# Moving half of a weight conversion from the attention stage to GpSimd behind it, with smaller input transfers

## The reference

```python
x = x + tanh(g_xattn[0]) * xattn(layernorm(x), ctx, ctx)   # x 32x128x512, ctx 32x128x128
x = x + tanh(g_ffn[0])   * moe(layernorm(x), weights)
# xattn: 32 query heads over 8 key/value heads of width 16, softmax over 128 keys; no projections
# moe, for each of the 4096 tokens:
gate  = xt @ Wr + br                       # 7 routed experts; top 2 of gate + gate_bias
probs = softmax of the two chosen gates
u = xt @ Wup[e] + bup[e]                   # 512 x 512
g = silu(u @ Wgate[e] + bgate[e]) * u      # 512 x 512
y = g @ Wdown[e] + bdown[e]                # 512 x 512
out = sum over the two chosen e of probs * y, plus the same three layers of one shared expert for every token
```

## Time and profile before

| | us |
|---|---|
| median of 3 runs | 1272.61 (1270.43 to 1278.21) |
| span of the profiled execution | 1271.7 |
| attention (to the first `norm2`) | 0 to 352.5 |
| norm stage (to the first expert matmul) | 352.5 to 407.5 |
| expert tiles | 407.5 to the end |
| busy: PE 1197.0, DVE 852.9, ACT 585.5, POOL 382.3 | |

### The profile page before, as it was taken

How to read it: one execution, slowest core, us unless ns; L and a number is a source line. 1 busy time by engine, 2 the same in 40 slices (tenths; PEclk the granted TensorE clock), 3 DMA queues, 4 the chain that set the end, 5 groups by cost and what they waited for, 6 DMA issues and landing times.

```text
span 1271.7 us, 40424 instructions
## 1 busy us (share of the span) xinstructions
PE 1197.0 (94%) x15162; PEld 889.3 (70%) x15162; DVE 852.9 (67%) x1470; ACT 585.5 (46%) x1131; POOL 382.3 (30%) x454
## 2 busy tenths in 40 slices
PE   3878889999878999999999999999999999999998
PEld 2544444555467777778888888888888888877775
DVE  5889989999887789445554455444444444447899
ACT  2767779898797422233333333333333333322221
POOL 4466766676830000210111111111111111006752
PEclk9888999999989999999999999999999999999999
DMA  5675555656665132644322454215412233057875
GB/s 183 211 247 176 176 172 187 212 186 212 209 252 190 52 133 67 225 152 152 119 82 82 139 183 157 66 58 193 146 66 66 66 125 123 33 175 234 265 227 176
DMA packets 91043, 196.32 MB, mean 154 GB/s; under 512 B 12128, under 2 KB 12640, under 8 KB 90976
## 3 DMA queue, kind: packets, MB, share of 16 engines
q1 hardware_dynamic: 80256, 160.30, 36.8%
q0 software_dynamic: 10720, 35.14, 9.2%
HBM read 331.68 MB, written 64.49 MB: 312 GB/s over the span
## 4 chain that ended last, share of the span: by engine, by line
PE 73%; DVE 12%; issue 5%; POOL 3%; DMA 3%; ACT 2%; SPq 1%; DVEq 1%; ACTq 0%; POOLq 0%
PE PS L1671 40%; PE PS L1709 20%; DVE negm L1011 5%; PE PS L1632 3%; PE PS L1484 3%; DMA qB<-negT 2%; PE PS L1518 2%; PE PS L1504 1%; ACT x2n L881 1%; POOL whl L696 1%; PE PS L1532 1%; DMA wr<-in_wr 1%; PE PS L1526 1%; DVE X L1314 1%; DVE rec L1024 1%
## 5 line engine op out<-in xcount | busy, mean ns | idle before, releaser
L1671 PE MATMUL PS<-xT,wb 128*128 128x128 f16 (+1 forms) x4128 | 279.8, 229 | 2.3 <-DVE gate L1152 1.6
L1671 PE MATMUL PS<-uhl,wb 128*128 128x128 f16 (+1 forms) x4128 | 279.8, 229 | 1.2 <-DVE uhl L1265 1.2
L1671 PEld LDWEIGHTS PS<-xT,wb 128*128 128x128 f16 x4128 | 264.1, 98 | 11.2 <-DVE gate L1152 1.7
L1671 PEld LDWEIGHTS PS<-uhl,wb 128*128 128x128 f16 x4128 | 263.5, 98 | 10.1 <-DVE uhl L1265 1.4
L1709 PE MATMUL PS<-wb,ghl 128*128 128x512 f16 x1200 | 267.2, 379 | 0.0
L1709 PEld LDWEIGHTS PS<-wb,ghl 128*128 128x128 f16 x1200 | 115.9, 98 | 130.2
L926 ACT ACTIVATE sl<-PS,bb 128x128 f32<-128x128 f32 (+1 forms) x344 | 106.7, 387 | 187.5 <-PE PS L1671 187.5
L747 POOL COPY ixr<-idx 128x2 int32 (+1 forms) x35 | 6.4, 183 | 593.3 <-PE PS L1632 593.3
L916 ACT ACTIVATE u<-PS,bb 128x128 f32<-128x128 f32 (+1 forms) x344 | 106.6, 387 | 169.5 <-PE PS L1671 164.1
L1272 DVE TENSOR_TENSOR g<-sl,u 128x512 f32<-128x512 f32 x102 | 70.5, 691 | 150.2 <-ACT sl L926 150.1
L1011 DVE TENSOR_REDUCE negm<-PS 128x8 f16<-128x1024 f32 x128 | 155.2, 1213 | 23.8 <-PE PS L1484 23.0
(11 more groups left out here) (161 smaller groups left out, 1375.9 us busy)
## 6 DMA issues: line engine op xcount, KB each, us to landing
wb<-wsc SPq DMA_DIRECT2D x219, 1024.0 KB
wst<-in_wall SPq DMA_DIRECT2D x32, 768.0 KB, 6.0
wsc<-whl SPq DMA_DIRECT2D x32, 768.0 KB, 4.3
ysl<-yb SPq DMA_DIRECT2D x43, 512.0 KB
bd<-in_bdown SPq DMA_DIRECT2D x74, 256.0 KB
X<-in_x SPq DMA_DIRECT2D x8, 1024.0 KB, 6.7
qB<-qT SPq DMA_DIRECT2D x32, 256.0 KB, 2.7
xnd<-xhl SPq DMA_DIRECT2D x32, 256.0 KB, 2.0
```

Source lines behind the costliest of these rows:

```text
L1671: ins = pe.matmul(bank_of(bank, t, m, kind), wb[:, j, l, k, w, m * P:(m + 1) * P], rhs(x, k)[:, ts], start=(n == 0), stop=(n == len(TERMS) ...
```

## The change

- Only 15 blocks (`DURING`) are converted in attention, one in every second body. Times 64 goes from DVE to POOL there (`weights64` in odd bodies), the high piece stays on ACT (odd bodies), the low piece on POOL (even bodies).
- The other 17 blocks are converted after attention by POOL alone (`late_block`: times 64, cast, subtract), through new tiles `wst2` and `whl2` that lie where `wb` buffer 1 will be. SP loads two of them ahead, and stores and loads between the `store_x2` of groups 2 to 7 (one block each) and between the tiles 0 to 4 (2, 2, 2, 2, 3 blocks).
- Buffer 1 of `wb` is therefore needed later: tiles 0 to 6 use buffer 0 and tile 7 buffer 1; the shared expert's second load and the first routed expert's loads move back by a tile or more.
- X arrives in 16 transfers of 2 batches (512 KB) where there were 8 of 4; the pairs from the sixth on are issued one in each body. ctx arrives in three transfers where there were two.

```diff
+XP = NB // 2
+DURING = NB // 2 - 1
+KEPT_C = (0, 4, 14, NB)
...
+        with ExitStack() as spare:
+            sb("first_half", [P, 3 * KT * 2 * HID], F16, spare)
+            wst2 = sb("wst2", [P, 2, 3, HID], F32, spare)
+            whl2 = sb("whl2", [P, 2, 3, 2, HID], F16, spare)
...
             if kind == "early":
-                return 1 if isinstance(half, int) and half == SH_A // 2 - 1 else 0
+                return 1 if isinstance(i, int) and i == SH_A - 1 else 0
...
+                    sp.dma_start(X[:, 2 * c:2 * c + 2, :], xv[:, 2 * c:2 * c + 2, :]).then_inc(x_in[c], 16)
...
-                if isinstance(half, int) and number(half, par) + 3 < XC:
-                    load_rows([number(half, par) + 3])
-                if not start:
-                    pv = (half - 1, 1) if par == 0 else (half, 0)
-                    store_w(*pv, nx is None)
+                if isinstance(half, int) and number(half, par) + 5 < XP:
+                    load_rows([number(half, par) + 5])
+                if isinstance(half, int) and number(half, par) == 5:
+                    load_ctx(2)
+                if par == 1 and not (isinstance(half, int) and half == 0):
+                    store_w(half, quad)
...
+            sp.wait_ge(S["t_done"], UNITS * NB)
+            for n in range(DURING, DURING + 2):
+                load_late(n)
+            late = iter(range(DURING, NB))
+            for i in range(NB // 4):
                 store_x2(i)
+                if i > 1:
+                    store_late(next(late))
...
+                for n in range(0, 0 if i == 5 else 3 if i == 4 else 2):
+                    store_late(next(late))
+                if i == 5:
+                    for j in range(2):
+                        sp.wait_ge(w_out[j], 16 * (NB // 2))
+                    for l in range(3):
+                        first_layer(l, 1)
                 store_y(i, i % 2)
...
+            def late_block(n):
+
+                j = n % 2
+                g.wait_ge(w_in[j], 16 * (n // 2 + 1))
+                g.tensor_scalar(wst2[:, j, :, :], wst2[:, j, :, :], WS, None, ALU.mult).then_inc(S["w64_ready"], 1)
+                g.wait_ge(S["w64_ready"], n + 1)
+                g.wait_ge(w_out[j], 16 * (n // 2))
+                g.tensor_copy(whl2[:, j, :, 0, :], wst2[:, j, :, :]).then_inc(S["whi_ready"], 1)
+                g.wait_ge(S["whi_ready"], n + 1)
+                g.tensor_tensor(whl2[:, j, :, 1, :], wst2[:, j, :, :], whl2[:, j, :, 0, :], ALU.subtract).then_inc(S["wlo_ready"], 1)
...
-                if not start:
-                    weights_lo(*pv)
+                if par == 0 and not start:
+                    weights_lo(half - 1, 1 - weight_block(half, quad)[0])
+                if par == 1 and not (isinstance(half, int) and half >= DURING):
+                    weights64(half, quad)
...
             residual(NB // 2 - 1, 1)
-            weights_lo(NB // 2 - 1, 1)
+            g.wait_ge(S["pv_done"], 2 * NB)
+            late_block(DURING)
             rstd2(3)
+            for n in range(DURING + 1, NB):
+                late_block(n)
...
-                weights64(half, par)
```

More of the change, by code:

```diff
@@ L201, in program @@
         qB_in = [sem(f"qB_in{j}") for j in range(2)]
-        x_in = [sem(f"x_in{c}") for c in range(XC)]
-        c_in = [sem(f"c_in{c}") for c in range(2)]
+        x_in = [sem(f"x_in{c}") for c in range(XP)]
+        c_in = [sem(f"c_in{c}") for c in range(3)]
         w_in = [sem(f"w_in{j}") for j in range(2)]
@@ L369, in neg_rows, with stored_block, store_w, load_late @@
                 sp.dma_start(qB[D::STRIP, par, pair, :, :], negT[:, pair, :]).then_inc(neg_in[pair], 16)
[L371 to L378, removed]
+            def stored_block(n, pieces, j):
+                sp.wait_ge(S["wlo_ready"], n + 1)
+                sp.dma_start(wsc[bass.ds(block_of(n), 1)].rearrange("o l p r -> (o p) l r"),
+                             pieces[:, j, :, :, :].rearrange("p l h c -> p l (h c)")).then_inc(w_out[j], 16)
+            def store_w(half, quad):
+                j = 1 - weight_block(half, quad)[0]
+                stored_block(half - 1, whl, j)
+                if not (isinstance(half, int) and half + 1 >= DURING):
+                    load_w(half + 1, j)
+            def load_late(n):
+                sp.dma_start(wst2[:, n % 2, :, :], a["wall"][block_of(n)]).then_inc(w_in[n % 2], 16)
+            def store_late(n):
+                stored_block(n, whl2, n % 2)
+                if n + 2 < NB:
+                    load_late(n + 2)
             queries_again(0, 0, 0)
@@ L821, in evac_o, with weights_hi @@
                 act.activation(oT[:, hf, :], AT, ACT.Copy).then_inc(S["oT_ready"], 1)
[L823 to L829, removed]
+            def weights_hi(half, quad):
+                j, count = weight_block(half, quad)
+                act.wait_ge(S["w64_ready"], half + 1)
+                need(act, w_out[j], count)
+                act.activation(whl[:, j, :, 0, :], wst[:, j, :, :], ACT.Copy).then_inc(S["whi_ready"], 1)
             act.wait_ge(S["vone"], 7)
@@ L851, in body @@
                 exps(half, par, 0)
-                if isinstance(half, int) and number(half, par) == 1:
-                    act.wait_ge(c_in[1], 16)
+                for c in (1, 2):
+                    if isinstance(half, int) and number(half, par) == KEPT_C[c] - 3:
+                        act.wait_ge(c_in[c], 16)
                 if later is not None:
@@ L865, in body @@
                 exps(half, par, 3)
-                if not (isinstance(half, int) and number(half, par) == NB - 1):
-                    weights_hi(half, par)
+                if par == 1 and not (isinstance(half, int) and half >= DURING):
+                    weights_hi(half, quad)
             over_batches(act, body)
@@ L960, in stats1 @@
             def stats1(c):
-                v.wait_ge(x_in[c], 16)
+                for pair in range(2 * c, 2 * c + 2):
+                    v.wait_ge(x_in[pair], 16)
                 for b in range(c * n, (c + 1) * n):
@@ L969, in late_stats1 @@
             def late_stats1(c, pair, one):
-                if pair == 0 and one == 0:
-                    v.wait_ge(x_in[c], 16)
+                if one == 0:
+                    v.wait_ge(x_in[2 * c + pair], 16)
                 b = c * n + 2 * pair + one
```

72 lines of the change are left out of this document (33 added, 39 removed).

## The result

| | before | after |
|---|---|---|
| median, us | 1271.52 (4 runs, 1270.21 to 1278.21) | 1364.62 (4 runs, 1363.22 to 1368.31) |
| ratio | | 1.0713, 95% interval 1.0677 to 1.0748 |
| attention | 352.5 | 338.6 (-13.9) |
| norm stage | 55.0 | 93.8 (+38.8) |
| tiles 0 to 5, up to the gate of tile 6 | 110.2 | 175.5 (+65.3) |

The change makes the kernel 7.1% slower. The direction, and where the time goes, are as forecast (-18, +19, +28), but the amount is 90 us of span (93 between the medians) and not 29. The boundaries are read from the timeline: the first `norm2` on ACT, the first expert matmul on PE, and PE's gate products of tile 6. The profiled stretches are one run each. In the ratios of this document executions far above the rest are left out (one of small_rows_lo_thirds, 2299.6 us, and one of the kernel before beside it, 2908.2).

What follows compares the result with a forecast made beforehand. Early attention was taken as bound by waits, its loop by nearly full PE, DVE and ACT, the norm stage by ACT, expert tiles by PE. Forecast: 1271.7 - 18 + 19 + 28 = 1300.7, stated as 1300 us; range 1256 to 1330.

Steps and rivals of the forecast that it cites:

- Small transfers, -4: Attention, early bodies: smaller X and ctx transfers shorten waits for negT, body 5 gets a new pile; -4 us (-10 to +1).
- Early pairs, -10: Attention, six pairs of bodies up to the twelfth: key split and DVE's chain shorten without DVE's times 64; 6 x 1.7 = -10.
- the loop, -4: Attention, other 16 bodies: DVE relieved, but PE nearly full, so 0.25 us gained a body; -4 (0 to -11).
- What one late block costs, 1.5 + 1.5 + 3.1: POOL behind attention: times 64, cast and subtraction of one block take 6.1 us, 17 blocks 104 us.
- Rival (c): POOL's one-operand instructions cost 3.1 like the subtraction, a block 9.3, DVE loses half as much again; 1329 us, chance 0.15.
- What it costs DVE: Behind attention: DVE's two-SBUF-operand instructions stop until POOL's instruction ends, extrapolated from 0.5 us waits to whole 3.1 us instructions.
- Norm stage, +19: Norm stage: a group with a block becomes 3.4 us longer by blocking, about 5.5 blocks; +19 (+9 to +28).
- Tiles, +28: Tiles 0 to 4: a block costs DVE about 4.5 us, less DVE's idle time, all passed to PE; +28 (+12 to +45).
- Routed tiles and the later reloads, 0: After the late blocks: tile 7's weights and the routed loads have a tile of cover each; +0, at most +3.
- POOL would keep ahead of SP: SP's queue: with 6.1 us a block, POOL finishes late blocks before SP's queued stores need to wait for them.
- (a): Behind attention: blocking is no loss, POOL falls into DVE's idle and PSUM time, only transfers count; 1263 us, chance 0.16.
- (b): No blocking loss, attention at its better bound (-28) as the clock rises, transfers hidden (+3); 1247 us, chance 0.12.

Runs made afterwards that it cites:

- small_rows_lo_thirds: Kernel before with small X and ctx transfers, all times 64 on POOL in two-operation form, low-piece subtraction cut in thirds: 1277.0 us, ratio 1.0018.
- fast64: The change with POOL's times 64, in attention and behind it, in the two-operation form (times 64, plus 0.0) on one row of 1536: 1329.2 us.
- late_empty: The change with each late block's three POOL instructions shrunk to two columns, all transfers kept, last 17 blocks stored as zeros: 1273.6 us.

## Why the prediction was wrong in its amount

Each step against what it measured:

- **Small transfers, -4.** By themselves 0.6 in the profile; the runs leave -4.1 to +1.5, so that -4 is at the edge of what they allow. The pile that I had put on body 5 came: the chain of the changed kernel has one transfer of `negT` left in the early bodies, of 7.31 us, in that body.
- **Early pairs, -10, and the loop, -4.** Attention gained 13.9 for a forecast of 18. The loop alone gave more than its term: 8.84 us a body (252.10 - 216.73 over 4), where I had 9.0, so 16 x 0.4 = 6.4. The other 7.5 lie in the early bodies (by POOL's thirteenth addition to X, at 181.33 and before at 188.61, the change is 7.3 ahead), and not 14. Both shares are of one run and known to a few us. The key split fell to 0.40 as I had said.
- **What one late block costs, 1.5 + 1.5 + 3.1.** This is the step that failed first: times 64 took 4.2, outside the bounds of 1.4 to 3.1. I had priced it by the memset, because "both read one operand" (a memset reads none), and took the subtraction as an upper bound, because it reads two. Neither bounds it. fast64 puts its weight at 34 us. Rival (c) had half of the mechanism: it made both one-operand instructions cost 3.1, where times 64 cost 4.2 and the cast 1.5. That its block of 9.3 us is near the measured 9.1 is luck, and its 1329 was still too low for a measured 1364.6. The Trainium skill's rule for one input (GPSIMD Engine Reference, "4.1 Engine selection"), by which a block was to stay near 6.1, holds for the cast and the two-operation form and not for this one.
- **What it costs DVE: it stops until POOL's instruction is over.** Right, and so was the extrapolation to a whole long instruction: 3.47 for 0.69 beside a POOL subtraction of 3.15. It is not exact for the slow times 64, beside which DVE was done 0.33 us before the end, twice.
- **Norm stage, +19.** Measured +38.8, made of 14.8 for the transfers, 11.0 for blocking with a block of 6.6 us, and 13.0 more with the slow times 64. I had worked out both blocking (19) and transfers (9) and took the larger, as if one hid the other. It does not: fast64 grew by 25.8, which is more than the 14.8 of the transfers and more than the 17.1 us that DVE stood (64.1 - 47.0). They do not add up in full either, as far as DVE's 17.1 is the measure of blocking; a run with blocking and no transfers is missing. The transfers alone were under-sized, 9 for 14.8. DVE's loss was over-sized, 17.1 / 7 = 2.4 us a block in fast64 for my 4.0, and the blocks were seven and not 5.5. The 13.0 are the size of times 64 again.
- **Tiles, +28.** Measured +65.3, of which 43.9 (154.7 - 110.9, from late_empty) remain in fast64. The share that I gave to DVE was nearly right: 4.5 of each 6.1 us, 45 for ten blocks; measured 137.8 - 88.5 = 49.3. What failed is the way from DVE's loss to the stretch. I took nine blocks, subtracted DVE's idle time (12.6 us over tiles 0 to 4), and had no term for PE's clock. By the table above PE's waits in fast64 grew by 30.7, which is near my 28 (32.4 with the tenth block), and 13.9 more are PE's own products, which take longer behind each wait. So one account is that the idle time did cover what I said and the missing term is the clock. Seen from DVE it is another: in all five kernels the stretch grew by about what DVE stood, and its idle time in the stretch hardly fell (21.6 before, 16.9 in fast64), as if it bought little, since a stop in front of `uhl` shifts PE, PE shifts ACT, and DVE waits again. Slower products also leave DVE more idle time, and no run holds the clock up, so which of the two it is stays open. What is shown is the sum, DVE's added time almost one to one, and the clock's 13.9 in it, which the prediction put at nothing.
- **Routed tiles and the later reloads, 0.** Right: 753.7 against 754.0.

That transfers for tile 7 were covered and that blocking is what decides the sign held. That POOL would keep ahead of SP held but for two blocks in the tiles, for which SP waited 7.6 and 15.1 us (5.1 and 12.6 in fast64); no wait of PE is put down to it. Of the signs, `low2` above 2 us came, the groups of the norm stage took about 11 us and not 9 (POOL's times 64 at 401.70, 412.49 and 423.59), and tile 2, from gate to gate, 32.6 and not 24. Rivals (a) and (b) are out by late_empty against the change: 91 us apart with the same transfers. Still open is why the one-operation form is slow, and how the 7.5 us of the early bodies divide between keys and DVE.

## What to carry to other kernels

- Spare time on GpSimd is not spare if VectorE works from SBUF at the same time. Price a moved instruction by what VectorE loses while it runs. In a stage that is a loop of PE, ACT and DVE waiting for each other, count that loss almost in full: here the stage grew by about what VectorE stood, and a part of that was TensorE's slower clock behind each wait (13.9 of 44.6 us in fast64). A block brought about 0.8 us where it was taken out (13.9 / 17, small transfers included), and cost 3.7 (norm stage, 25.8 / 7, its transfers included) to 4.4 (tiles, 43.9 / 10) where it was put, even in its fast form.
- An instruction that the trace does not show need not be bounded by a neighbour that does more work. Measure it first; one run with four forms would have shown the factor of 2.6.
- Where such work must lie beside VectorE, cut it in short pieces on the engine that has time (16 us here), and do not take the larger of transfers and blocking for the whole: 25.8 us here, with 14.8 for the transfers alone and 17.1 that VectorE stood.

## What the runs showed of the hardware

- GpSimd's tensor_scalar with one operation on 1536 float32 columns takes 4.1 to 4.4 us whatever its shape, type of output (4.24 into float16) or source of the factor. With a second operation it takes 1.48 to 1.54 in attention and 1.62 to 1.70 behind it, as fast as the cast (1.53 to 1.66), and faster than the product with a broadcast tile (2.90).
- VectorE's two-input subtraction ended 0.54 to 0.55 us after a GpSimd addition or subtraction that it had to wait for (0.69 grew to 3.47), but 0.33 us before the end of the one-operation `tensor_scalar`, twice.
- A GpSimd instruction that only writes leaves VectorE's two-input instructions alone (694 and 703 ns beside it) and holds up its casts (526 ns for 426).
- VectorE gets in between GpSimd instructions that stand back to back, and then GpSimd waits: its 512-column subtraction took 1.40 us in the mean behind attention where a third of 3.33 is 1.11, and `low2` fell from 1279 to 909 ns in the mean.
